# Layer A's normed rows, transposed by the host instead of by TensorE, in a two-layer graph-attention kernel

## What is computed

```python
scores = einsum('bqhd,bkhd->bhqk', q, k) * scale + 2 * adj      # layer A: 12 heads of 32
p = softmax(scores);  out = einsum('bhqk,bkhd->bqhd', p, v) @ Wo.T + bo
x = x + out                                                      # q, k, v from layernorm(x)
x = x + mixture_of_three_heads(layernorm(x))                     # layer B: 3 heads of 128, causal,
                                                                 # a gate that keeps two, then Wp
```

## Time and profile before

| | before |
|---|---|
| median of 3 runs | 2238.44 us (2238.24 to 2240.43) |
| the profiled execution: its time | 2238.38 us |
| the profiled execution: its span | 2236.3 us |
| TensorE busy | 2201.6 us, 98% of the span |
| VectorE busy | 1903.9 us, 85% |
| ScalarE busy | 1500.0 us, 67% |
| GpSimd busy | 1157.3 us, 52% |
| mean granted TensorE clock | 0.995 of full speed |
| HBM read, written | 39.18 MB, 25.17 MB |

### The profile page before, as it was taken

The page is one execution under the profiler, slowest core; times in us unless marked ns, Lnnn a source line. Parts: engine busy times, 40 slices in busy tenths (PEclk is TensorE's granted clock), DMA queues, the critical chain, the costliest instruction groups (busy, mean ns, idle before and its releaser), DMA issues.

```text
span 2236.3 us, 51593 instructions
## 1 busy us (share of the span) xinstructions
PE 2201.6 (98%) x16941; PEld 1439.2 (64%) x16941; DVE 1903.9 (85%) x7152; ACT 1500.0 (67%) x5298; POOL 1157.3 (52%) x1551
## 2 busy tenths in 40 slices
...
DMA packets 142265, 143.20 MB, mean 64 GB/s; under 512 B 16816, under 2 KB 141360, under 8 KB 142000
## 3 DMA queue, kind: packets, MB, share of 16 engines
q1 hardware_dynamic: 139808, 138.62, 23.3%
...
HBM read 39.18 MB, written 25.17 MB: 29 GB/s over the span
## 4 chain that ended last, share of the span: by engine, by line
PE 94%; DVE 2%; SPq 1%; POOL 1%; issue 1%; DMA 0%; ACT 0%; DVEq 0%; POOLq 0%
PE B_bank L517 33%; PE A_bank L517 32%; PE A_bank L597 7%; PE A_bank L609 4%; PE B_bank L616 4%; PE A_bank L584 4%; PE B_bank L591 4%; PE B_bank L601 2%; PE A_bank L560 2%; PE B_bank L560 2%; SPq L492 1%; DVE raw_score L957 1%; DVE smax L963 0%; DMA Ks<-k_hi 0%; POOL S L1096 0%
## 5 line engine op out<-in xcount | busy, mean ns | idle before, releaser
L712 ACT ACTIVATE S<-raw_score,smin 128x128 f32<-128x128 f32 x1536 | 593.9, 393 | 172.9 <-DVE smin L957 172.9
L1096 POOL TENSOR_TENSOR S<-S,rowf 128x512 f32<-128x512 f32 x384 | 389.1, 1041 | 314.8 <-DVE rowf L982 314.8
L957 DVE CUSTOM_DVE_ANT_0 raw_score<-A_bank,adj,s_unit 128x128 f32<-128x128 f32 x1536 | 444.7, 346 | 4.3 <-PE A_bank L584 1.5
L1101 POOL TENSOR_TENSOR S<-S,row2f 128x384 f32<-128x384 f32 x128 | 106.0, 828 | 612.1 <-DVE row2f L990 611.9
L726 ACT ACTIVATE PT<-A_bank 128x512 f32<-128x512 f32 x384 | 220.1, 590 | 234.9 <-PE A_bank L597 234.9
L712 ACT ACTIVATION_READ_ACCUMULATOR S<-raw_score,smin 128x1 f32 x1536 | 296.0, 193 | 0.0
L597 PE MATMUL A_bank<-ident,S 128*128 128x128 f32 x1536 | 226.7, 274 | 3.6 <-DVE smin L957 2.5
L963 DVE TENSOR_REDUCE smax<-raw_score 128x12 f32<-128x1536 f32 x128 | 223.0, 1742 | 0.0
L597 PEld LDWEIGHTS A_bank<-ident,S 128*128 128x128 f32 x1536 | 187.0, 141 | 41.4 <-DVE smin L957 3.4
L719 ACT ACTIVATE S<-S,s2min 128x128 f32<-128x128 f32 x384 | 148.4, 390 | 3.0 <-DVE s2min L967 3.0
L584 PE MATMUL A_bank<-Ks,Qs 96*128 96x128 f16 x1536 | 140.6, 221 | 7.7 <-DMA Ks<-k_hi 5.0
...
## 6 DMA issues: line engine op xcount, KB each, us to landing
xin<-in_x SPq DMA_DIRECT2D x32, 768.0 KB, 4.5
Qs<-q_hi SPq DMA_DIRECT2D x256, 96.0 KB, 2.2
out<-x1res SPq DMA_DIRECT2D x128, 192.0 KB, 2.1
Ks<-k_hi SPq DMA_DIRECT2D x252, 96.0 KB, 2.3
Qs<-q_lo SPq DMA_DIRECT2D x128, 96.0 KB, 2.2
Ks<-k_lo SPq DMA_DIRECT2D x126, 96.0 KB, 2.3
adj<-in_adj SPq DMA_DIRECT2D x32, 256.0 KB, 3.4
...
```

The source lines that it names most:

```text
L712: ins = nc.scalar.activation(S[b % 2][:, h, :], raw_score[:, h, :], ACT.Exp, bias=smin[b % 2][:, h:h + 1], scale=-1.0, accum_out=ssum[b % ...
L957: ins = nc.vector.tensor_tensor_reduce(raw_score[:, h, :], src[:, j * T:(j + 1) * T], adj2[:, b, :], s_unit[:], 3.0e38, ALU.add, ALU.min, ...
L1096: nc.gpsimd.tensor_tensor(S[b % 2][:, hs, :], S[b % 2][:, hs, :], rowf[b % 2][:, hs].unsqueeze(2).broadcast_to([P, HPC, T]), ALU.mult).the ...
L1101: nc.gpsimd.tensor_tensor(S2[b % 2][:], S2[b % 2][:], row2f[b % 2][:].unsqueeze(2).broadcast_to([P, NE, T]), ALU.mult).then_inc(normed2, 1)
```

## The change

1. From group 2 on, TensorE transposes nothing for layer A. The host passes `x` a second time as `xT`, with channels on the partitions. SyncE loads it into `xt` (new step `A.xT`, 768 KB per group). `xt` takes the place of `h1`; groups 0 and 1 still go the old way, in the same memory.
2. Mean and reciprocal deviation now lie along the free dimension, so they must be spread over all partitions. GpSimd still makes them (`statistics1`), now into `stat`. SyncE writes them to DRAM as `stat_rows` (new step `A.stat`, 128 x 8 single f32 elements) and reads them back as `stat_wide` for all 128 partitions (new step `A.rows`).
3. GpSimd adds and multiplies: `A.hx.0` to `A.hx.2`, two products with 128x512 elements each, in the place of four 128x384 operations.
4. ScalarE and VectorE make `hT_hi` and `hT_lo` from `xt` in SBUF and not from a PSUM bank. The ring of five banks is no longer used by these steps.
5. `xin` has two tiles; `A.res` loads the group after next. The second tile is loaded at the start of the program, ahead of the third weight.
6. The orders of all engines in `ORDER_OF_STEPS` are written anew. `A.ln1` stands first in VectorE's and GpSimd's turn, `A.v.0` first in TensorE's; on SyncE the load of `x` now stands between the two stacks. `LAST_STEPS` is unchanged.

```diff
     "pool": """
-        W.adj.0@0 A.res.0@0 A.res.1@0 A.res.2@0 A.res.3@0 A.ln1@0 W.lo.4@0 W.lo.5@0 A.norm.0@0 A.norm.1@0
+        W.adj.0@0 A.res.0@0 A.res.1@0 A.res.2@0 A.res.3@0 A.ln1@0 A.h1@1 W.lo.4@0 W.lo.5@0 A.norm.0@0 A.norm.1@0
...
     "pe": """
...
+        A.v.0 A.score.0.0 A.v.1 A.score.0.1 B.hT.0 B.hT.1 B.hT.2 A.score.0.2 A.v.2 A.score.1.0 A.v.3 A.score.1.1
+        B.qk.0 A.score.1.2 B.v.0 B.qk.1 B.v.1 B.qk.2 A.turn.0.0 A.turn.0.1 A.score.2.0 A.score.2.1 B.v.2 B.v.3
+        A.turn.0.2 B.qk.3 B.qk.4 A.mix.0 A.turn.1.0 A.turn.1.1 B.qk.5 A.turn.1.2 A.proj.0 B.score.0 B.score.1
+        A.score.2.2 A.qk.0 A.qk.1 A.score.3.0 A.qk.2 A.mix.1 B.turn.0 B.score.2 A.score.3.1 B.turn.1 B.mix.0
+        A.qk.3 B.score.3 B.mix.1 A.score.3.2 B.proj.0 A.turn.2.0 A.turn.2.1 A.qk.4 A.turn.2.2 A.qk.5 A.proj.1
+        A.mix.2 B.turn.2 B.proj.1 A.turn.3.0 B.mix.2 A.turn.3.1 A.turn.3.2 B.turn.3 A.proj.2 A.mix.3 B.mix.3
+        B.proj.2 A.proj.3 B.proj.3
...
     "dve": """
...
+        A.ln1 A.v.0 A.score.0.0 A.v.1 A.score.0.1 B.hT.0 B.hT.1 B.hT.2 A.score.0.2 A.v.2 A.v.3 A.smax.0 B.v.0
+        A.norm.0 A.score.1.0 A.score.1.1 A.score.1.2 B.v.1 B.conv A.smax.1 B.v.2 B.v.3 A.norm.1 A.score.2.0
+        B.gate.0 A.score.2.1 A.mix.0 A.hT.0 B.gate.1 A.hT.1 B.score.0 A.hT.2 A.proj.0 B.gate.2 B.score.1
...
     "pool": """
-        A.res.0 A.res.1 A.res.2 A.res.3 A.norm.0 A.ln1 B.res.0 B.res.1 B.res.2 B.res.3 A.norm.1 B.norm.0
-        B.norm.1 A.norm.2 B.norm.2 A.norm.3 B.norm.3 A.ln2.0 A.ln2.1 A.adj A.ln2.2 A.ln2.3
+        A.ln1 B.res.0 A.res.0 A.res.1 B.res.1 A.norm.0 B.res.2 A.hx.0 A.norm.1 A.hx.1 A.hx.2 B.res.3 B.norm.0
+        B.norm.1 A.norm.2 B.norm.2 A.res.2 A.res.3 A.norm.3 B.norm.3 A.ln2.0 A.ln2.1 A.adj A.ln2.2 A.ln2.3
     "sp": """
-        A.res A.stack.0 A.adj A.stack.1 B.proj.0 B.proj.1 B.proj.2 B.proj.3
+        A.stat A.rows A.stack.0 A.adj A.res A.stack.1 B.proj.0 B.proj.1 B.proj.2 A.xT B.proj.3
...
+def turned(step, g):
+
+    return step[:2] == ("A", "hT") and g >= TURNED
...
 def ahead(step):
-    return step[0] == "A" and step[1] in ("hT", "qk", "stack")
+    return step[0] == "A" and step[1] in ("hT", "qk", "stack", "xT", "stat", "rows", "hx")
...
+TURNED = 2
...
-        xin = sb("xin", [P, GB, C])
+        xin = [sb(f"xin{k}", [P, GB, C]) for k in range(2)]
         xres = sb("xres", [P, GB, C])
-        h1 = sb("h1", [P, GB, C])
+        xt = sb("xt", [P, KC, GB * T])
+        h1 = xt[:].rearrange("p c n -> p (c n)").rearrange("p (b n) -> p b n", b=GB)
+        stat = [sb(f"stat{k}", [P, 2, GB]) for k in range(2)]
+        stat_wide = sb("stat_wide", [P, 2, GB * T])
...
             sp.dma_start(rows[1][1], rows[1][0].unsqueeze(0).broadcast_to([P, C])).then_inc(bo_loaded, 16)
+            sp.dma_start(xin[1][:], dram_group(x, 1)).then_inc(x_loaded[1], 16)
             load_raw(2)
...
-                if (stage, kind) == ("A", "res") and not last:
+                if (stage, kind) == ("A", "res") and g + 2 < NG:
 
                     sp.wait_ge(xres_ready, count(g, GB, GB))
...
-                    sp.dma_start(xin[:], dram_group(x, following(g))).then_inc(x_loaded, 16)
+                    sp.dma_start(xin[g % 2][:], dram_group(x, g + 2)).then_inc(x_loaded[g % 2], 16)
+                if (stage, kind) == ("A", "xT") and not last:
+
+                    if following(g) == TURNED:
+                        wait_products(sp, ("A", "hT", KC - 1, 0), g)
+                    else:
+                        wait_evacuated(sp, ("A", "hT", KC - 1, 0), g)
+                    sp.dma_start(xt[:], xT[following(g)]).then_inc(xT_loaded, 16)
+                if (stage, kind) == ("A", "stat"):
+                    sp.wait_ge(rstd1_done, count(g, 1, 1))
+                    sp.dma_start(stat_rows[g].rearrange("q b t -> t q b"), stat[g % 2][:],
+                                 allow_slow_non_contiguous=True).then_inc(stat_stored, 16)
+                if (stage, kind) == ("A", "rows"):
+
+                    sp.wait_ge(stat_stored, count(g - TURNED, 16, 16))
+                    if g > TURNED:
+                        sp.wait_ge(hx_ready, count(g - TURNED, KC, 0))
+                    sp.dma_start(stat_wide[:], stat_rows[g].rearrange("q b t -> q (b t)").unsqueeze(0)
+                                 .broadcast_to([P, 2, GB * T])).then_inc(stat_spread, 16)
...
+                elif kind == "hT" and A and g >= TURNED:
+                    act.wait_ge(hx_ready, count(g - TURNED, KC, b + 1))
+                    if b == 0:
+                        wait_products(act, ("A", "v", GB - 1, 0), before(g))
+                        wait_products(act, ("A", "qk", 2 * KC - 1, 0), before(g))
+                    nc.scalar.activation(hT_hi["A"][:, b, :], xt[:, b, :], ACT.Copy, scale=H_SCALE)\
+                        .then_inc(hi_ready["ahead"], 1)
...
-                    nc.vector.scalar_tensor_tensor(out=hT_lo[stage][:, b, :], in0=src[:, :], scalar=H_SCALE,
+                    rows_T = xt[:, b, :] if turned(step, g) else src[:, :]
+                    nc.vector.scalar_tensor_tensor(out=hT_lo[stage][:, b, :], in0=rows_T, scalar=H_SCALE,
...
+                elif kind == "hx":
+                    if b == 0:
+                        pool.wait_ge(xT_loaded, count(g - TURNED, 16, 16))
+                        pool.wait_ge(stat_spread, count(g - TURNED, 16, 16))
+                    nc.gpsimd.tensor_tensor(xt[:, b, :], xt[:, b, :], stat_wide[:, 0, :], ALU.add).then_inc(centred, 1)
+                    pool.wait_ge(centred, count(g - TURNED, KC, b + 1))
+                    nc.gpsimd.tensor_tensor(xt[:, b, :], xt[:, b, :], stat_wide[:, 1, :],
+                                            ALU.mult).then_inc(hx_ready, 1)
```

More of the change, by code:

```diff
@@ L120 @@
     "sp": """
-        A.res@0 A.stack.0@0 A.stack.1@0 A.stack.0@1 A.adj@0 A.stack.1@1
+        A.res@0 A.stack.0@0 A.stack.1@0 A.stack.0@1 A.adj@0 A.stack.1@1 A.xT@1
     """,
@@ new lines @@
+        A.score.1.2 A.turn.0.0 B.qk.2 A.turn.0.1 A.turn.0.2 A.score.2.0 A.hT.0 A.mix.0 B.qk.3 A.turn.1.0
+        B.gate.0 B.qk.4 A.turn.1.1 B.qk.5 A.hT.1 A.score.2.1 A.hT.2 B.gate.1 A.turn.1.2 B.score.0 A.qk.0
+        B.score.1 A.qk.1 A.score.2.2 B.turn.0 B.mix.0 A.mix.1 A.qk.2 B.turn.1 B.score.2 A.qk.3 A.score.3.0
+        A.turn.2.0 A.score.3.1 A.turn.2.1 A.score.3.2 A.turn.2.2 B.mix.1 A.qk.4 A.qk.5 B.score.3 A.mix.2
+        B.turn.2 B.mix.2 A.turn.3.0 A.turn.3.1 A.turn.3.2 B.turn.3 A.mix.3 B.mix.3
```

81 lines of the change are left out of this document (41 added, 40 removed).

## The result

| | before | after |
|---|---|---|
| median (4 runs each, same chip) | 2238.34 us | 2255.65 us (2255.03 to 2262.26) |
| ratio | 1 | 1.0084, 95% interval 1.0063 to 1.0104 |
| span of the profiled execution | 2236.3 us | 2254.1 us |
| a turn | 68.17 us | (2088.1 - 95.8) / 29 = 68.70 us |

The change makes the kernel slower by 0.8%, 17 us, where 2201.3 us was forecast. One run of a later kernel (halves with `B.res.3` late), 2510.59 us at a mean granted clock of 0.85, is left out of that kernel's median, which would be 2216.15 us with it. In `after` and its descendants `A.turn` is line 626, `A.hx` lines 1174 and 1176, B.gate's products line 915, the low parts of `hT` line 968.

The account below looks back on a forecast made before the run. TensorE's own work was taken to bound every turn. From the 2236.3 us span, 39.6 us go, 1.5 for the start and 1 for small waits come: 2199.2, plus 2.1 outside the span, 2201.3 us; range 2194 to 2224.

Parts of the forecast that it names:

- What bounds the kernel: Whole turn: TensorE's own work sets the time in all 30 turns, 68.17 us each.
- the price of what goes: TensorE: three `A.hT` steps fewer per turn at 0.44 us, 39.6 us in all, leaving turns of 66.85 us.
- The rest is whether the new order feeds it: TensorE's new list, walked by the chain's prices: inputs should arrive in time, such as `hT_lo` with 0.8 us to spare.
- Six operations at 1.33: GpSimd's `A.hx`: six 128x512 operations of 1.33 us replace four of 0.90, adding 4.4 us per turn.
- only the place counts: GpSimd: with 32 us free, the added 4.4 us per turn matters only by where it stands.
- Rival 1: Shared port: VectorE's `hT_lo`, with two SBUF inputs, blocked by GpSimd's `A.hx`; 9 to 39 us, about 2220; chance 0.12.
- The moments: DRAM trip: `A.stat` 5.5 us, at most 7.3, hidden; slower rival at 0.165 us per piece, 2279 us, chance 0.07.
- K behind x: Load of x between stacks: fits with 1.1 us slack; rival loses 0.3 to 1.0 us per turn, 2210 to 2231, chance 0.10.
- The start and the small waits: Second `xin` load ahead of the third weight costs 1.5 us; small waits of the new order cost 1.
- the late spread: Upper-end time in the turn when the moments are spread over all partitions: 17.6 us, against 20.6 needed for `A.hx.0`.
- The smallest DMA: Trace's DMA of 128 pieces, said to land in 3.5 us; taken as the lower bound for `A.stat`.
- The slower side: Chance that the change makes the kernel slower: 0.07, against 0.05 for the same and 0.88 for faster.

Follow-up runs that it names:

- halves with `B.res.3` late: Changed kernel with each `A.hx` operation issued as two of 256 columns and GpSimd's `B.res.3` moved behind `B.norm.1`: 2215.91 us, ratio 0.9896 to before.
- one-tile: Changed kernel with `A.hx` taking one tile and two columns as operands, all rows normed by the first's moments: 2204.12 us.
- short `A.hx`: Changed kernel with the `A.hx` operations on 128 of 512 columns only, three quarters of the rows left un-normed: 2207.23 us.

## Why the prediction was wrong, point by point

- **What bounds the kernel, and the price of what goes: right.** The turn without holds is 66.97 to 67.06 us (the one-tile and the short `A.hx`) against 66.85 forecast.
- **"The rest is whether the new order feeds it": here it failed.** I walked TensorE's list only to the steps that the change touches, `A.qk` and the scores. `A.turn.1.2` isn't touched, but it stands between them, and its bank is emptied behind a step with two-operand instructions. Walked on with the prediction's own prices, TensorE asks for the bank some 29.9 us into the turn and VectorE, through with the gate as long as before, has emptied it at 29.1 (22.0 plus the 9.5 us that this took in after, less 2.3). The 2.3 us by which `A.hx` lengthens the gate, less these 0.8, are the 1.5 us of wait that were measured. The forecast cost this at nothing; it cost 1.8 us a turn, 55 us in all.
- **"Six operations at 1.33": right** (1.31 and 1.29), and nearly so GpSimd's total. That "only the place counts" was right as well. I asked only what GpSimd would be late for, not whom it would hold up while it was on time.
- **Rival 1: the right mechanism, the wrong instruction.** It placed the lock at `hT_lo`, 9 to 39 us. `hT_lo` did lengthen, to 906 ns on average, though only the first of the three, beside `B.res.3` and not beside `A.hx`, and it cost nothing in after: with `B.res.3` moved, all three are back at 683 ns and the time is the same. The same lock at `B.gate.0`, whose line 875 was the very row quoted for it, cost everything. Since two of its three products were held already before, it passed for a cost that was paid; the change put the third product and the two short instructions behind it under holds as well.
- **The moments: the size was off, the conclusion right.** From `A.stat` to `A.rows` it took 9.6 us in the median and 10.5 in the turn shown, against 5.5 taken and 7.3 as upper end. The price per piece was 0.15 us (estimated as above), not at most 0.060, and thus about the 0.14 from which the prediction would have called the kernel slower. That did not happen, because the spread has more room than I gave it (`A.hx.0` was done at 1006.65 of the turn shown, and `A.norm.1` was released at 1007.79), and without the trip the time is the same.
- **K behind x: right that nothing is lost.** K landed after 4.1 us instead of 2.3, and TensorE waited for it 0.7 us in all behind the start.
- **The start and the small waits: right.** The measured span, 2254.1, lies 54.9 us above the forecast one, 2199.2, and 30 x 1.85 us is 55.5. So both together cost 1.9 us, where 1.5 + 1 was taken.
- **Slips that decided nothing.** By its own terms the late spread stands at 17.2 us, not 17.6, and rival 1's low end at 0.6 us a turn, not 0.3. "The smallest DMA" of 3.5 us was the quickest of the small ones at the start and not the smallest; 4 KB in 128 pieces took 1.4 us.
- **The slower side** was given 0.07, all of it to the moments. The mechanism that decided it was in the text, with a chance of 0.12, but on the faster side.
